# A gated cross-attention block with a quantized MLP on one core: five banks for the first tiles of x, an early Gelu, and the last block of h in two halves

## The reference

```
x = x + tanh(g_xattn) * attention(layernorm(x), ctx, ctx)         # 16 heads of 32
x = x + tanh(g_ffn) * ffn(layernorm(x))

def quant(a):  s = max(|a|) / 127;  return round(a / s), s        # one s for the whole tensor
def ffn(x):
    xq, sx = quant(x); wq, sw = quant(w1)                         # w1: 2048 x 512
    h = gelu((xq @ wq.T + b1) * (sw * sx))
    hq, sh = quant(h); wq, sw = quant(w2)                         # w2: 512 x 2048
    return (hq @ wq.T + b2) * (sw * sh)
```

## Time and profile before

| what | us |
|---|---|
| median of 3 runs | 622.41 (622.37 to 625.25) |
| the profiled execution's span | 619.4 |
| start of the first tile of y | 372.33 |
| first rounding of h | 504.23 |
| last matmul's end | 616.14 |

### The profile page before, as it was taken

The page is one execution under the profiler, slowest core; times in us unless marked ns, Lnnn a source line. Parts: engine busy times, 40 slices in busy tenths (PEclk is TensorE's granted clock), DMA queues, the critical chain, the costliest instruction groups (busy, mean ns, idle before and its releaser), DMA issues. The chain is left out here.

```text
span 619.4 us, 9745 instructions
## 1 busy us (share of the span) xinstructions
PE 584.2 (94%) x3415; PEld 339.3 (55%) x3415; DVE 480.4 (78%) x690; ACT 328.0 (53%) x395; POOL 202.9 (33%) x175
## 2 busy tenths in 40 slices
PE   6999899999998999999989788999999989999997
PEld 5845657557566566575675475444444454444443
DVE  6968889978889788688675785989999788965361
ACT  2444365751743725527327236777776669544440
POOL 3125153632431712424108230000001809803473
PEclk9999899999999999999999999999999999999999
DMA  9922000460100100001001119877776969889753
GB/s 311 404 72 93 1 1 2 137 204 0 69 2 0 69 1 31 40 0 68 0 1 68 69 68 324 305 281 294 275 271 251 425 232 348 321 310 386 251 218 141
DMA packets 37188, 98.20 MB, mean 159 GB/s; under 512 B 2720, under 2 KB 3488, under 8 KB 32544
## 3 DMA queue, kind: packets, MB, share of 16 engines
q1 hardware_dynamic: 35808, 96.36, 41.5%
q10 hardware_dynamic: 1344, 1.37, 0.7%
HBM read 55.77 MB, written 41.94 MB: 158 GB/s over the span
## 5 line engine op out<-in xcount | busy, mean ns | idle before, releaser
L1233 PE MATMUL ps<-h_sb,w_q 128*128 (+1 forms) x488 | 109.6, 379 | 1.8 <-ACT xo L1295 1.8
L1497 PE MATMUL ps<-w_q,h_q 128*128 128x512 bf16 x448 | 96.9, 379 | 0.0
L1031 POOL TENSOR_TENSOR c_lo<-c_sb,c_hi 128x512 fp32r<-128x512 f32 x32 | 41.4, 1302 | 111.3 <-ACT c_hi L588 111.3
L1233 PEld LDWEIGHTS ps<-h_sb,w_q 128*128 128x128 bf16 x488 | 46.8, 98 | 53.8 <-ACT xo L1295 2.4
L1579 POOL TENSOR_TENSOR xo<-xo,b2s 128x512 f32<-128x512 f32 x32 | 56.4, 1795 | 60.5 <-DMA xo<-x_dram 42.0
L1497 PEld LDWEIGHTS ps<-w_q,h_q 128*128 128x128 bf16 x448 | 43.8, 98 | 52.9
L1295 ACT ACTIVATE xo<-ps,b1s,sc 128x1024 f32<-128x1024 f32 x48 | 57.6, 1204 | 20.0 <-PE ps L1233 19.0
L575 ACT ACTIVATE prob<-ps 77x1024 f32<-77x1024 f32 x64 | 61.6, 1012 | 7.7 <-PE ps L385 7.7
L1366 DVE TENSOR_REDUCE hmax<-xo 128x1024 f32 (+1 forms) x48 | 57.0, 1212 | 9.7 <-ACT xo L1295 9.7
L623 ACT ACTIVATE q_hi<-ps,bq_sb 128x512 fp32r<-128x512 f32 x32 | 22.0, 687 | 78.0 <-PE ps L343 77.9
L1040 POOL TENSOR_TENSOR x<-x,bo_gate 128x512 f32<-128x512 f32 (+1 forms) x32 | 41.5, 1310 | 49.3 <-DVE xn L742 33.4
(11 more groups left out here) (147 smaller groups left out, 1100.3 us busy)
## 6 DMA issues: line engine op xcount, KB each, us to landing
h_dram<-xo SPq DMA_DIRECT2D x48, 512.0 KB, 2.7
h_sb<-h_dram SPq DMA_DIRECT2D x16, 1024.0 KB, 11.0
x_dram<-x SPq DMA_DIRECT2D x8, 1024.0 KB, 3.9
xo<-x_dram SPq DMA_DIRECT2D x8, 1024.0 KB, 4.8
x<-h_dram SPq DMA_DIRECT2D x8, 1024.0 KB, 7.8
x<-in_x SPq DMA_DIRECT2D x7, 1024.0 KB, 5.5
out<-xo SPq DMA_DIRECT2D x7, 1024.0 KB, 4.4
x<-in_w_t SPq DMA_DIRECT2D x1, 4096.0 KB, 20.2
```

Of the source, the lines that this page charges most:

```text
L1031: nc.gpsimd.tensor_tensor(c_lo[:, g, :], c_sb[:, g, :], c_hi[:, g, :].bitcast(F32), ALU.subtract).then_inc(c_lo_on, 1)
L1233: mm = nc.tensor.matmul(ps[:, 2 * (m % 2) + s, :], w1_q[:, k, m * P:(m + 1) * P], xq_t[:, one(2 * j + s), k, :], start=(k == 0), stop=(k = ...
L1497: mm = nc.tensor.matmul(ps[:, 4 * s + t, :], h_q[s][:, m, t * P:(t + 1) * P], w2_q[:, m, :], start=(m == 0), stop=(m == MF - 1))
```

## The change

It has four parts.

- The eight first tiles go through five banks (4, 5, 1, 3, 7) instead of two. VectorE copies tiles 1, 3 and 6, ScalarE the others, each with a semaphore of its own (`words_dve`, `words_act`). TensorE makes four tiles, `half(0, 0)`, tiles 4 and 5, `half(1, 0)`, tiles 6 and 7, `half(2, 0)`. VectorE's copies 1 and 3 stand ahead of y4, copy 6 behind b1s.
- ScalarE does a Gelu of one column behind the last `c_copy` of the attention. Its result isn't used.
- The last block of h (last pair, m = 15) is multiplied with s outermost; Gelu and maximum are done for each half of 512 tokens, the second maximum in a new column of hmax.
- In `output` the output scale is worked out behind the sixteen roundings instead of ahead of them.

```
@@ program: hmax holds one column more (NC // 2 * MF + 1)
@@ attention, ScalarE, last pass of body(i, b, b_prev, prev, nxt)
                     if nxt is None:
                         c_copy(i - 1, GROUPS - 1, True)
+                        nc.scalar.activation(bk_sb[:, 0:1], sh.bq[:, 0:1], ACT.Gelu)
                         for g in range(GROUPS):
                             c_high(i - 1, g)
@@ hidden
+        WORD_BANKS = (T0, T1, 1, 3, TW)
+        BY_DVE = (1, 3, 6)
+
+        def words_copied(u):
+
+            by_dve = sum(v <= u for v in BY_DVE)
+            return (words_dve, by_dve) if u in BY_DVE else (words_act, u + 1 - by_dve)
+
+        def words(u):
+            return ps[:, WORD_BANKS[u % len(WORD_BANKS)], :].rearrange("p (k n) -> p k n", k=KD)
@@ hidden, TensorE
                     pe.wait_ge(xq_on, n - PT + 1)
-                    if not isinstance(n, int) or n >= 2:
-                        pe.wait_ge(xqt_on, n - 1)
+                    if not isinstance(n, int) or n >= PT + 2:
+                        pe.wait_ge(xqt_on, n - PT - 1)
...
                 def magic_words(u):
 
                     pe.wait_ge(y_on, u + 1)
-                    if u >= 2:
-                        pe.wait_ge(xqt_on, u - 1)
+                    if u >= len(WORD_BANKS):
+                        pe.wait_ge(*words_copied(u - len(WORD_BANKS)))
                     for k in range(KD):
-                        mm = nc.tensor.transpose(ps[:, T0 if u % 2 == 0 else T1, k * P:(k + 1) * P],
+                        mm = nc.tensor.transpose(ps[:, WORD_BANKS[u % len(WORD_BANKS)], k * P:(k + 1) * P],
                                                  y[:, u % YS, k * P:(k + 1) * P], sh.ident[:])
...
                 def half(m, s):
 
-                    if s == 0:
-                        pe.wait_ge(xqt_on, TT)
-                    else:
-                        pe.wait_ge(xqt_on, PT)
+                    pe.wait_ge(words_act, (PT if s else TT) - sum(u < (PT if s else TT) for u in BY_DVE))
+                    pe.wait_ge(words_dve, sum(u < (PT if s else TT) for u in BY_DVE))
...
                 def step(j, first, last):
                     if not first:
-                        pe.wait_ge(xqt_on, PT * j + PT)
+                        pe.wait_ge(xqt_on, PT * j)
...
+                        by_half = last and m == MF - 1
+                        for k, s in ([(k, s) for s in range(2) for k in range(KD)] if by_half else
+                                     [(k, s) for k in range(KD) for s in range(2)]):
...
+                            if by_half and k == KD - 1 and s == 0:
+                                mm.then_inc(h_mm, 1)
                         mm.then_inc(h_mm, 1)
...
-                for u in range(TT + 1):
+                for u in range(TT):
                     magic_words(u)
                 half(0, 0)
+                magic_words(4)
                 magic_words(5)
                 half(1, 0)
                 magic_words(6)
+                magic_words(7)
                 half(2, 0)
-                magic_words(7)
@@ hidden, ScalarE
-                        words = ps[:, T0 if u % 2 == 0 else T1, :].rearrange("p (k n) -> p k n", k=KD)
-                        nc.scalar.activation(dst, words, ACT.Copy, bias=-MAGIC).then_inc(xqt_on, 1)
+                        nc.scalar.activation(dst, words(u), ACT.Copy, bias=-MAGIC).then_inc(words_act, 1)
...
+                        if last and m == MF - 1:
+                            nc.scalar.activation(dst[:, 0:CH], ps[:, bank, :], ACT.Gelu,
+                                                 bias=b1s[:, m:m + 1], scale=sc[:, 4:5]).then_inc(h_on, 1)
+                            act.wait_ge(h_mm, MF * j + m + 2)
+                            nc.scalar.activation(dst[:, CH:2 * CH], ps[:, bank + 1, :], ACT.Gelu,
+                                                 bias=b1s[:, m:m + 1], scale=sc[:, 4:5]).then_inc(h_on, 1)
+                            continue
...
                 for u in range(PT):
-                    transposed(0, u)
+                    if u not in BY_DVE:
+                        transposed(0, u)
@@ hidden, VectorE
+                def copy_words(u):
+
+                    dve.wait_ge(xqt_mm, u + 1)
+                    nc.vector.tensor_scalar(xq_t[:, u // TT, :, (u % TT) * P:(u % TT + 1) * P], words(u), -MAGIC, 1.0,
+                                            ALU.add, ALU.mult).then_inc(words_dve, 1)
...
+                    if u == TT - 1:
+                        copy_words(1)
+                        copy_words(3)
...
                 nc.vector.tensor_scalar(b1s[:], sh.b1[:], sc[:, 4:5], None, ALU.mult).then_inc(xs_on, 1)
+                copy_words(6)
...
+                        if last and m == MF - 1:
+                            nc.vector.tensor_reduce(dst, src[:, 0:CH], AX.X, ALU.max,
+                                                    apply_absolute_value=True).then_inc(hmax_on, 1)
+                            dve.wait_ge(h_on, n + 2)
+                            nc.vector.tensor_reduce(hmax[:, n + 1:n + 2], src[:, CH:2 * CH], AX.X, ALU.max,
+                                                    apply_absolute_value=True).then_inc(hmax_on, 1)
+                            continue
@@ output, VectorE
                 nc.vector.reciprocal(hs[:, 3:4], hs[:, 2:3]).then_inc(hs_on, 1)
-                nc.vector.scalar_tensor_tensor(hs[:, 4:5], hs[:, 2:3], sh.sw2[:, 0:1], sh.gate[:, 1:2], ALU.mult,
-                                               ALU.mult).then_inc(hs_on, 1)
-                dve.wait_ge(hs_on, 5)
+                dve.wait_ge(hs_on, 4)
...
                 for m in range(MF):
                     src = h_kept[:, m, 0, :]
                     nc.vector.tensor_scalar(src, src, hs[:, 3:4], MAGIC, ALU.mult, ALU.add).then_inc(h_rnd_first, 1)
+                nc.vector.scalar_tensor_tensor(hs[:, 4:5], hs[:, 2:3], sh.sw2[:, 0:1], sh.gate[:, 1:2], ALU.mult,
+                                               ALU.mult).then_inc(hs_on, 1)
+                dve.wait_ge(hs_on, 5)
                 nc.vector.tensor_scalar(b2s[:], sh.b2[:], hs[:, 4:5], None, ALU.mult).then_inc(hs_on, 1)
```

More of the change, by code:

```diff
@@ L84, in program @@
         sh.sw2 = keep("sw2", [P, 1])
-        sh.hmax = keep("hmax", [P, NC // 2 * MF])
+        sh.hmax = keep("hmax", [P, NC // 2 * MF + 1])
         sh.x1_out = sem("x1_out")
@@ L1139, in hidden @@
         xqt_on = sem("xqt_on")
+        words_act = sem("words_act")
+        words_dve = sem("words_dve")
         h_mm = sem("h_mm")
@@ L1230, in step @@
                             pe.wait_ge(h_on, MF * j + m - 1)
-                        for k in range(KD):
-                            for s in range(2):
-                                mm = nc.tensor.matmul(ps[:, 2 * (m % 2) + s, :], w1_q[:, k, m * P:(m + 1) * P],
-                                                      xq_t[:, one(2 * j + s), k, :], start=(k == 0),
-                                                      stop=(k == KD - 1))
+                        by_half = last and m == MF - 1
+                        for k, s in ([(k, s) for s in range(2) for k in range(KD)] if by_half else
+                                     [(k, s) for k in range(KD) for s in range(2)]):
+                            mm = nc.tensor.matmul(ps[:, 2 * (m % 2) + s, :], w1_q[:, k, m * P:(m + 1) * P],
+                                                  xq_t[:, one(2 * j + s), k, :], start=(k == 0),
+                                                  stop=(k == KD - 1))
+                            if by_half and k == KD - 1 and s == 0:
+                                mm.then_inc(h_mm, 1)
                         mm.then_inc(h_mm, 1)
```

## The result

| | kernel before | changed kernel |
|---|---|---|
| median | 624.34 us (10 runs, 622.37 to 625.25) | 621.89 us (10 runs, 619.46 to 622.83) |
| the profiled execution | not told | 622.26 us, span 620.4 |

The ratio is 0.9963, with a 95% interval of 0.9946 to 0.9981: 0.37% faster, within the 0.5% that was called no change, though the interval does not reach 1. The forecast was 0.43% less and 619.7 us. The difference came out, 2.45 us against 2.70, and the time did not: it lies 2.2 us above the forecast and outside the range that ended at 621.4. One execution among the later repetitions of the kernel before, 633.75 us at a mean granted clock of 0.94, was in a slower state of the chip and is left out of every ratio.

What follows compares the result with a forecast made beforehand. TensorE, busy 94% of the span, was taken to bound the kernel, so earlier matmuls bring the end forward. Terms 0.84 + 1.28 + 0.45 + 0.13 = 2.70 us off 622.41 gave 619.7 us, range 618.4 to 621.4.

Steps and rivals of the forecast that it cites:

- A: Start of the MLP: five banks and two copying engines bring the second halves from 380.93 to 380.09, 0.84 us.
- B: First Gelu of the MLP: an early one-column Gelu moves the table load into ScalarE's idle time, saving 1.28 us.
- C: End of h: the last block by halves lets VectorE's last maximum end at 501.86 instead of 502.31, 0.45 us.
- D: Start of the output: the output scale moved behind the roundings lets the first rounding start 0.13 us sooner.
- rival 3: Table load at the first Gelu: ScalarE empties before a switch, 1.1 us more would go, 618.6 us; chance 0.04.
- rival 1: Table load stays or returns at the first real Gelu, 621.0 us, or 622.3 if Identity needs another set; chance 0.08.
- rival 2: Ring of h writes held by w2's load: Gelu 4 waits 0.9 us for its slot, 620.6 us; chance 0.06.
- the median of the runs is 622.41: Whole kernel before: the measured level from which the forecast gain of 2.70 us was subtracted, giving 619.7 us.
- 3.0 us: Around the profiled span: difference between the 622.41 us median and the 619.4 us span, taken as unchanged.
- in 9 to 12 us PE worked 0.43 of 3 us and the clock stayed 1.00: Early in the kernel: a little-worked TensorE stretch without a clock fall, cited against the rival of a falling clock.
- Rival 4: TensorE's clock falls to 1.2 GHz at its gap from 374.8 to 375.75 in the MLP, 626.7 us; chance 0.04.
- Covered by 10 us: Output: scale and b2s some 0.25 us later; GpSimd's fourth addition done near 522.5, TensorE wants the bank at 533.2.

Runs made afterwards that it cites:

- the filled idle stretches: Empty TensorE transposes added in three idle stretches of the attention: on the changed kernel 619.61 us, ratio 0.9939 to before; on the kernel before 622.84 us.
- the scale in the middle: Changed kernel with the output scale worked out behind the fourth of sixteen roundings: 621.28 us, ratio 0.9959; with the empty transposes too, 619.76 us, ratio 0.9941.
- the store first: Changed kernel with SyncE's store of the second chunk's output issued ahead of four loads of h: 620.69 us, ratio 0.9952.

## Why the prediction was wrong, and where it was right

**Parts A to D as terms.** All four came out close to the sum, read within the profile up to the first rounding:

| term | forecast | alone | in the changed kernel |
|---|---|---|---|
| A | 0.84 | 0.88 | |
| B | 1.28 | 1.27 at the first Gelu, 0.99 at the first rounding | |
| A and B | 2.12 | | 2.17 |
| C | 0.45 | 0.51 | |
| D | 0.13 | 0.13 | |
| sum to the first rounding | 2.70 | | 2.82 |

Alone the four give 0.88 + 0.99 + 0.51 + 0.13 = 2.51 us, together 2.82; nearly all of the difference is the 0.28 us that part B lost alone. C was a little more than forecast because the two maxima of 512 columns follow every 0.60 us and not every 0.67. VectorE's copy was 0.691 where 0.69 was taken. The load's drain, rival 3, did not show: 1.27 us went, not 2.66. Identity and copies ran behind the early Gelu with no third load, which ends rival 1. The ring was never held: the Gelu of m = 4, the first to reuse a slot, and the 24 behind it each stand 2.17 us nearer to y0 than before, as the first one does, which ends rival 2.

**The step that failed first** is the level from which the sum was subtracted: "the median of the runs is 622.41", with "the median itself is uncertain by some tenths". Ten runs of the same kernel had a median of 624.34, and later ones 623.55, 624.32 and 623.77, between 621.06 and 625.21. So three runs were too few for the level, and about 1.5 us was right where the range took in some tenths. That alone puts the result outside a range that ends at 621.4: 624.34 - 2.70 = 621.64. The "3.0 us" around the span come from the same mistake, though the forecast time does not rest on them; 1.9 to 2.1 lie around it, and the profile was of an execution near 621.4 us. As a difference the forecast held at first (0.37%, interval 0.19 to 0.54, against 0.43) and not in the repetition (0.20%, 0.07 to 0.33). By the segments the change is worth 2.82 us less what the end gives back, 0 to 0.81 in its profiles. That 2.45 came so near to 2.70 is in part luck: the sum had no term for the end, and its other terms were 0.12 too low.

**The second** is "Against it: in 9 to 12 us PE worked 0.43 of 3 us and the clock stayed 1.00". It was one draw. At the same place the clock fell in the changed kernel's profile, from 12 to 15 us at 0.50, and stayed at 1.00 when that kernel was run again. The length of the idle stretch ahead of it did not decide: TensorE had stood 3.12 us before 11.57 in the kernel before, where the clock stayed, and 2.27 us before 11.56 in the changed kernel, where it fell. And the very profile that the argument drew on had a fall, near 72 us (0.83 over 70 to 80), where TensorE had stops of 1.19 and 1.54 us. Rival 4 had placed the fall at PE's new gap of 1 us in the MLP; there it stayed at 1.00 in every profile (the mean of 360 to 620 us in the changed kernel's is 1.00). The clock was one of the right suspects for the level, at the wrong place and not as a cost of the change.

**The third** is "Covered by 10 us", for b2s, and with it the condition "as long as the other engines keep up", which was checked for GpSimd's first additions only. TensorE indeed never waited for b2s. But moving the scale changed which of VectorE and GpSimd got through at 511 us, and the effect arrived 100 us later, through loads of x that went out up to 5.3 us later. Up to 0.82 us of the gain went there in single profiles. Over whole executions it can't be told: with part D the ratios are 0.9963 and 0.9980, without it 0.9962, and the intervals overlap.

Open is whether the pattern turns by the order of scale, wait and b2s or by b2s's delay, why part B alone lost 0.28 us inside h, and whether the meeting of VectorE and GpSimd near 114 us, set by an edit, would make the two values of that stretch.

A version that beats both kernels is the changed one with the filled idle stretches: 619.61 us, 0.6% less than before and 2.4 us less than the changed kernel run beside it (621.98). With the scale in the middle its profile had an end free of GpSimd; with the store first it was not run.

## What to carry to other kernels

When the gain in question is a few tenths of a per cent, forecast the difference and give the level the spread of many executions; then judge each part on segments within the profile: from y0 to the first rounding they repeated within 0.02 us, while whole executions spread over 4. Look at the spread the same way: cut the profiles into stretches and see which of them has two values. When an operation is moved on VectorE, look at what GpSimd does beside it: here one addition stood for 10.45 us or passed in 2.1, and the effect can come out at the far end through a store and the load that waits for it. In a DMA list, try the store that frees a buffer ahead of loads that are not yet urgent; here it landed 9.6 us sooner behind its issue, and the medians don't show what that is worth.

## What was not expected of the hardware

- A single GpSimd addition of 128x512 that takes 1.23 us alone took 10.45 while VectorE did eight roundings of 128x2048 at 1.28; when the engines took turns it was 2.2 and 2.04.
- Where VectorE's multiplication of 128x512 started 0.02 to 0.06 us ahead of GpSimd's addition, it took 0.69 and the addition 1.8; where it started level or up to 0.75 us behind, it took 1.08 to 1.82 and the addition 1.27. The first order made the stretch 28.1 us, the second 29.25, in all twelve profiles without a fall of the clock there.
- TensorE's granted clock fell from 1.00 to 0.50 in some executions and not in others of the same program: near 11.5 us it fell at idle times of 2.27 to 3.68 us and stayed at 3.07 to 3.25; near 355 us the idle time was 2.11 us whether it fell or stayed. A fall cost from nothing (near 72 us) to 2.5 us (near 12 us).
- A store of 1 MB took 18.1 to 21.1 us to land behind four loads of 1 MB that were issued just before it, and 11.3 ahead of them.
